# Making delta times u on VectorE, straight into the product bank, instead of on GpSimd with a copy behind it

## The reference, cut to what matters

```
xz    = x @ W_in;  x_in, z = split(xz)
u     = silu(conv(x_in) + conv_b)                 # 512 channels
delta = softplus(dt_lr @ W_dt + b_dt)             # 512 channels
dA    = exp(delta[..., None] * A)                 # 16 states a channel
dBu   = (delta * u)[..., None] * Bm[:, :, None, :]
h     = dA_t * h + dBu_t                          # over time
y_t   = sum over the states of h * C_t
out   = ((y + D_skip * u) * silu(z)) @ W_out
```

## Time and profile before

| | us |
|---|---|
| median of 3 runs | 1124.95 (1122.94 to 1130.54) |
| profiled execution | 1126.54 |
| its span, first to last instruction | 1124.8 |

### The profile page before, as it was taken

The page is one execution under the profiler, slowest core; times in us unless marked ns, Lnnn a source line. Parts: engine busy times, 40 slices in busy tenths (PEclk is TensorE's granted clock), DMA queues, the critical chain, the costliest instruction groups (busy, mean ns, idle before and its releaser), DMA issues.

```text
span 1124.8 us, 16949 instructions
## 1 busy us (share of the span) xinstructions
PE 936.3 (83%) x4574; PEld 636.9 (57%) x4575; DVE 1037.5 (92%) x1304; ACT 866.9 (77%) x1841; POOL 880.8 (78%) x570
## 2 busy tenths in 40 slices
PE   4946766587979999689988999899979999878866
PEld 3424434454656656556656765576647665556555
DVE  6999999799999988997899979999999999898894
ACT  4574788464897799667998699979997798976971
POOL 6268999599777877858787888887796896778895
PEclk9968977598999999799998999899988998889987
DMA  9586569953484535824457543764367343854313
GB/s 309 189 327 233 161 194 305 314 179 90 121 292 135 113 104 153 291 50 93 117 176 264 114 125 83 267 184 85 85 215 262 72 94 95 287 165 109 71 20 66
DMA packets 119367, 185.86 MB, mean 165 GB/s; under 512 B 12012, under 2 KB 104344, under 8 KB 111016
## 3 DMA queue, kind: packets, MB, share of 16 engines
q1 hardware_dynamic: 87120, 144.60, 37.8%
q0 software_dynamic: 19584, 25.26, 12.7%
q10 hardware_dynamic: 12568, 14.93, 4.2%
HBM read 146.34 MB, written 42.60 MB: 168 GB/s over the span
## 4 chain that ended last, share of the span: by engine, by line
PE 39%; issue 16%; ACT 15%; POOL 12%; DVE 10%; DMA 3%; ACTq 3%; SPq 1%; POOLq 0%; DVEq 0%
POOL hc L657 8%; PE psY L1142 7%; DVE hb L1637 7%; PE psA L1169 5%; PE psC L1232 4%; PE psC L1282 4%; ACT hb L842 3%; PE psA L1217 3%; PE psE L1259 3%; PE psA L1161 2%; ACT hnT L963 2%; POOL xs_d L672 2%; DMA Cb<-bc_d 2%; DVE psB L1626 1%; POOL out L706 1%
## 5 line engine op out<-in xcount | busy, mean ns | idle before, releaser
L657 POOL TENSOR_TENSOR hc<-hb,Cb 128x1024 f32<-128x1024 f32 x246 | 624.4, 2637 | 92.3 <-PE psY L1142 75.3
L1637 DVE TENSOR_TENSOR_SCAN hb<-hb,carry,psB 128x512 f32<-128x512 f32 x384 | 472.6, 1266 | 12.6 <-ACT hb L842 10.9
L1142 PE MATMUL psY<-ident,hc 128*128 128x128 f32 x2048 | 309.3, 293 | 78.3 <-POOL hc L657 78.2
L842 ACT ACTIVATE hb<-delta,aneg 128x512 f32<-128x512 f32 x512 | 351.5, 716 | 24.9 <-POOL hc L657 19.1
L1142 PEld LDWEIGHTS psY<-ident,hc 128*128 128x128 f32 x2048 | 257.7, 151 | 191.5 <-POOL hc L657 109.2
L1626 DVE TENSOR_TENSOR psB<-Bb,psU 128x512 f32<-128x512 f32 x510 | 324.3, 682 | 0.1
L706 POOL DMA_INDIRECT out<-yo,idx x80 | 128.0, 1600 | 60.2 <-DMA out<-yo,idx 25.0
L1637 DVE TENSOR_TENSOR_SCAN hb<-hb,psB 128x512 f32<-128x512 f32 x128 | 149.5, 1204 | 2.3 <-ACT hb L842 2.3
L1169 PE MATMUL psA<-ux,dgw 128*128 128x512 f32 x232 | 113.9, 610 | 3.0 <-ACT ux L782 1.2
L1282 PE MATMUL psC<-w2r,hnT 128*128 128x256 f32 x320 | 88.3, 423 | 0.0
L1259 PE MATMUL psE<-w1r,xgT 128*128 128x256 f32 x320 | 84.6, 410 | 0.0
(11 more groups left out here) (234 smaller groups left out, 1234.9 us busy)
## 6 DMA issues: line engine op xcount, KB each, us to landing
Bb<-bc_d SPq DMA_DIRECT2D x32, 1024.0 KB
Cb<-bc_d SPq DMA_DIRECT2D x32, 1024.0 KB
w1r<-w1c_d SPq DMA_DIRECT2D x80, 256.0 KB
w2r<-in_L_ffn_W SPq DMA_DIRECT2D x80, 256.0 KB
xg<-xs_d SPq DMA_DIRECT2D x20, 516.0 KB
xg<-xn_d SPq DMA_DIRECT2D x37, 128.0 KB
Bb<-in_L_attn_x SPq DMA_DIRECT2D x8, 512.0 KB, 8.3
xn_d<-hb SPq DMA_DIRECT2D x8, 512.0 KB, 8.1
```

The lines of the kernel that those rows point to most:

```text
L657: pool.tensor_tensor(hc[:, k:k + 2, :], hb[:, g % HR:g % HR + 2, :], Cb[:, n:n + 2, :], ALU.mult).then_inc(s_g, 1)
L842: act.activation(hb[:, g % HR, :], delta[:, dc, :], ACT.Exp, scale=aneg[:, dc, n:n + 1]).then_inc(s_exp, 1)
L1142: mm = pe.matmul(y[:, tt * P:(tt + 1) * P], hc[:, g % GR, tt * P:(tt + 1) * P], ident[:, :], start=False, stop=(n == NS - 1), is_transpose ...
L1637: dve.tensor_tensor_scan(h, h, psB[g % 2][:, :], first, ALU.mult, ALU.add).then_inc(s_scan, 1)
```

## The change

GpSimd's `du_mul` and its places in the tables go, and so does the semaphore s_du. VectorE's `du_copy` becomes a `tensor_tensor` of delta and u with `psU` as output, in the same place of its program. ScalarE's `x_in` now waits for VectorE's operation instead of GpSimd's.

```
-    "du": [53, 0, 23, 26],
...
-            def du_mul(p, dc):
-                j = p * DC + dc
-                pool.wait_ge(s_delta, j + 1)
-                pool.wait_ge(s_dup, j)
-                if j == 1:
-                    pool.wait_ge(s_dbu, 2)
-                pool.tensor_tensor(du[:, :], delta[:, dc, :], u_of(p, dc), ALU.mult).then_inc(s_du, 1)
...
-                        if c + 1 < NC:
-                            for _ in at(c, "du", s, 0, 1):
-                                du_mul(c + 1, 0)
-                        for dc in at(c, "du", s, 1):
-                            du_mul(c, dc)
...
-                    if j > UR:
-                        act.wait_ge(s_du, j - UR)
-                    else:
-                        act.wait_ge(s_dup, 1)
+                    act.wait_ge(s_dup, j - UR + 1)
...
-            def du_copy(j):
-
-                dve.wait_ge(s_du, j)
+            def du_mul(j):
+
+                dve.wait_ge(s_delta, j + 1)
                 dve.wait_ge(s_dbu, j * NS)
-                dve.tensor_copy(psU[:, :], du[:, :]).then_inc(s_dup, 1)
+                dve.tensor_tensor(psU[:, :], delta[:, j % DC, :], u_of(j // DC, j % DC), ALU.mult).then_inc(s_dup, 1)
```

More of the change, by code:

```diff
@@ L96 @@
     "d0_max": [3, 4, 7],
-    "du": [50, 7, 20, 32],
     "z_mm": [18, 18, 23, 24],
@@ L110 @@
     "d_max": [39, 52, 56, 6],
-    "du": [59, 5, 10, 29],
     "z_mm": [8, 19, 24, 24],
@@ L391, in build @@
         s_cl = [sem(f"s_cl{q}") for q in range(NS // NQ)]
-        s_dm, s_de, s_dl, s_delta, s_du, s_dup, s_dsk = (sem(n) for n in (
-            "s_dm", "s_de", "s_dl", "s_delta", "s_du", "s_dup", "s_dsk"))
+        s_dm, s_de, s_dl, s_delta, s_dup, s_dsk = (sem(n) for n in (
+            "s_dm", "s_de", "s_dl", "s_delta", "s_dup", "s_dsk"))
         s_zm, s_zc, s_z, s_gate = sem("s_zm"), sem("s_zc"), sem("s_z"), sem("s_gate")
@@ L1661, in _ @@
                     if (g0 + 2) % NS == 0 and g0 + 2 < NU:
-                        du_copy((g0 + 2) // NS)
+                        du_mul((g0 + 2) // NS)
                     scan(g0 + 1)
```

## The result

The changed kernel takes 1131.02 us (median of 4 runs, 1129.82 to 1132.71), the kernel before 1123.95 us in the runs beside them. The ratio is 1.006, with a 95% interval of 1.0031 to 1.0088. A second comparison, with 12 runs, gave 1.0058 (1.0036 to 1.008). So the change costs some 7 us, 0.6%: clearly more than nothing and less than 1%. The forecast was 1134 us.

What follows compares the result with a forecast made beforehand. Two engines were near full in each stretch, VectorE busiest but not alone on the path. -3.9 + 0.1 + (10.6 to 12.9) + 1 gave +9 us on 1126.54, 1135.5, less 1.6 above the median: 1134 us, range 1128 to 1141.

Steps and rivals of the forecast that it cites:

- The sum: Whole kernel: -3.9 + 0.1 + (10.6 to 12.9) + 1 = +7.8 to +10.1, taken as +9 us.
- The relief of GpSimd: GpSimd's 31 removed multiplications, 44.7 us busy: only six pieces on the chain count, a gain of 3.9 us.
- The operation alone: VectorE's multiplication in place of the copy, 692 against 675 ns: 0.5 us in all, 0.1 us on the chain.
- The wait inside the operation: VectorE's two-SBUF-input instruction at the seams waits for GpSimd's multiplication in flight: 25.1 us in sum, at most 29.6.
- How much reaches the end: VectorE's seam delays shrink by each idle gap they meet; 10.6 to 12.9 us reach the end.
- the delays that I counted in full: VectorE delays at 301, 529 and 567 (at 584), 661, 693, 756 and 785, 817, 1077 us: 12.9 us.
- GpSimd held in turn: VectorE's new multiplications hold GpSimd, mainly at 6 seams up to 280 us: about 2 us, 1 us on the path.
- Rival 1: All of VectorE's delay counts, as the absorbing gaps would move along: 1149 to 1152 us; chance 0.22.
- Rival 2: VectorE's instruction and GpSimd's multiplications hardly meet at the seams, GpSimd being more often in step: 1123 us; chance 0.18.
- Rival 3: GpSimd's relief wins, 16 us from eleven multiplications up to 325 and after 985 us: 1112 us; chance 0.08.
- Rival 4: Longer life of delta and u makes ScalarE wait: forecast plus some us, 1138 us; chance 0.04.
- the signs: Expected in the profile: VectorE's longest near 2.8 us, 20 to 30 us over copies, GpSimd's line 657 waiting longer for TensorE.

Runs made afterwards that it cites:

- two-step kernel: Changed kernel, but VectorE copies delta into psU between the two scans, then multiplies psU by u in place after the second: 1124.05 us, ratio 0.9981.

## Why the prediction was right

- *The sum.* +9 us was forecast, +7 measured. Both terms that carry it were measured apart. Their sizes came out close; for the second, in part by luck, as said below.
- *The relief of GpSimd*, taken from the pieces of its multiplications on the chain: 3.9 us. Measured: 4 us (1.8 to 6.3) from below, 5 from above. Reading the chain instead of the 44.7 us of busy time was what counted, though the interval is wide.
- *The operation alone*: nothing on the path forecast, nothing measured (662 ns at least).
- *The wait inside the operation*, read from the earlier trace rows: 25 to 29.6 us forecast, 33 measured. The number of meetings was right: 22 to 24 seams forecast, 23 measured, though not the same seams. The size is near by two errors of opposite sign. By my rule (what is left of the multiplication in flight, less 0.13 us), laid over the trace after, the waits would be some 20 us: less was left at the meetings than in the trace before. And at five seams VectorE waited for a further multiplication too, some 13 us in all, which the rule leaves out. The trace before had shown this. Of VectorE's ten multiplications by C, the one of 3710 ns began 0.27 us ahead of GpSimd's multiplication, while an indirect DMA was being issued, and still ended 1.09 us after it:

```profile
88.99 3.71 DVE L1646 TENSOR_TENSOR hc<-hb,Cb 128x1024 f32<-128x1024 f32 x1
...
88.27 0.96 POOL L672 DMA_INDIRECT xs_d<-xg,slots  x1 [0.30 <-issue]
89.26 2.35 POOL L657 TENSOR_TENSOR hc<-hb,Cb 128x1024 f32<-128x1024 f32 x1
```

- *How much reaches the end*: 10.6 to 12.9 of 29.6 us forecast, about two fifths; measured 10.8 of 33, a third. The kernel with the same delays and no contention at the seams shows that VectorE's delays are the price. It does not show why two thirds of them vanish. That they fall into VectorE's idle gaps is what I argued, and the shrunken waits fit it, but no run tests it, and the two-step kernel, where a tenth of 21 us arrives, speaks against a constant share. The agreement is luck in part: of the delays that I counted in full, those at 301, 529 and 817 us did not occur in the trace after (0.66 to 0.67 us at 304, 532 and 825), and the one near 661 was 3.5 us instead of 1.3.
- *GpSimd held in turn*: 1 us forecast, smaller than what these runs can tell. Single issues of DMAs were held, as the last section shows.
- *Rival 1* (all counts) fell: VectorE's waits shrank by 27 us. *Rival 2* (they hardly meet) was right in part: GpSimd is more often in step (64.3 us of waiting for the scans, from 15.8), and less is left of its multiplications at the seams than in the trace before; but 23 of 31 still meet one. *Rival 3* (relief wins) had the right place and the wrong size, 16 us for 4. *Rival 4*: no wait of ScalarE's `x_in` for VectorE appears.
- Of the signs, three were wrong: VectorE's longest, 2.8 us forecast, was 4.48, by the second multiplication; the sum over the copies was 33 us, not 20 to 30; and GpSimd's line of multiplications by C (657, now 654) does not wait longer for TensorE (75.3 us before, 65.1 after) but for VectorE's scans.

## What to carry to other kernels

Before moving an elementwise operation onto VectorE beside a busy GpSimd, count its inputs in SBUF: with two it waits for GpSimd's multiplication in flight, and sometimes for the next as well; with one input in PSUM the same operation never waited here. Even a copy into PSUM first was cheaper than the wait (0.8% here). Price such a wait by laying the new instruction over the old trace, and then price what of it reaches the end apart: take off the idle gaps that it can fall into, and count on no fixed share (a third of 33 us here; of 21 us some 2, which can't be told from nothing). Busy time taken from an engine with slack was worth about what of it lay on the chain, here 4 of 45 us.

## What the runs showed of the hardware

- A VectorE multiplication of 128x512 with two SBUF inputs ends 0.55 to 0.57 us after the GpSimd multiplication that it waited for, in all 23 cases of the trace after.
- A GpSimd multiplication queued directly behind the one in flight can go ahead of a VectorE instruction that already waits: at 270.53 and 397.73 us VectorE waited 3.5 and 3.8 us. The Trainium skill (SBUF — State Buffer, Who interferes with whom) says that issue order decides who is blocked; by the starts of the spans these rows differ from it.
- The same happened behind the issue of an indirect DMA, at 1078.87 us after and at 88.99 us before, but not each time: at 182.90 us and at 184.47 us in the two-step kernel, both beside such an issue, VectorE took its plain 1.23 and 1.22 us. In the second a multiplication followed the issue directly. What decides is not shown.
- GpSimd's issue of an indirect DMA was held by VectorE's two-input instruction: 2.01 us instead of 1.01. In the changed kernel eight issues of the line that writes `out` took 1.81 to 1.93 us, each beside one of the 31; in the trace before none of its 80 took over 1.71.
